# Second attention of a convolution-attention-expert network: heads inside images, keys projected three tiles after queries, image 0's softmax weights formed during image 1

## The reference, cut to what matters

```python
q, k, v = jnp.reshape(qkv, (3, b, n, d, h))        # b=2, n=1024, d=128, h=8
score = jnp.einsum('bnqh,btqh->bnth', q, k) * d ** (-0.5)
attn = jax.nn.softmax(score, axis=1)               # over the queries n
av = jnp.einsum('bnnh,bnqh->bnqh', attn, v)        # only the diagonal of attn
out = av.reshape(b, n, d * h) @ W0 + b0
t = t + out; t = t + ffn(layer_norm(t))
```

## Time and profile before

| what | us |
| --- | --- |
| median of 3 runs (446.90 to 447.89) | 447.43 |
| the profiled execution: time | 447.12 |
| its span, first to last instruction | 445.4 |
| PE busy, of the span | 399.7 |
| DVE busy | 322.2 |
| ACT busy | 300.5 |
| POOL busy | 92.8 |

### The profile page before, as it was taken

One profiled execution on the slowest core, in us unless ns is written; L12 is line 12 of the kernel. 1 busy time (PEld: TensorE's weight loads), 2 busy tenths in 40 slices (PEclk: granted clock), 3 DMA queues, 4 the chain that ended last, 5 costly groups with the idle time before them and its releaser, 6 DMA issues.

```text
span 445.4 us, 6582 instructions
## 1 busy us (share of the span) xinstructions
PE 399.7 (90%) x1919; PEld 316.0 (71%) x1919; DVE 322.2 (72%) x697; ACT 300.5 (67%) x576; POOL 92.8 (21%) x121
## 2 busy tenths in 40 slices
PE   1989779969999999999999999999939999839995
PEld 1678776947888888888888888888825775726763
DVE  2788853327889888898889888898963557467555
ACT  1476684338989999999999999999851001637750
POOL 8600002023104221232132320423010110142000
PEclk9999998879999999999999999999985999958995
DMA  7940000000000000000000000000000000000002
GB/s 271 353 123 2 1 1 0 1 0 1 1 1 1 2 0 0 0 0 0 0 0 0 0 0 0 0 0 1 1 0 0 0 0 1 0 1 0 2 0 96
DMA packets 3877, 9.60 MB, mean 22 GB/s; under 512 B 530, under 2 KB 1682, under 8 KB 3730
## 3 DMA queue, kind: packets, MB, share of 16 engines
q1 hardware_dynamic: 3426, 8.39, 5.5%
q10 hardware_dynamic: 432, 0.97, 0.6%
HBM read 8.31 MB, written 1.05 MB: 21 GB/s over the span
## 4 chain that ended last, share of the span: by engine, by line
PE 79%; DVE 12%; issue 4%; ACT 2%; DMA 1%; POOL 0%; POOLq 0%; DVEq 0%; ACTq 0%
PE ps L998 12%; PE ps L1035 12%; PE ps L1037 12%; PE ps L1036 12%; PE ps L1080 6%; PE ps L942 3%; PE ps L950 2%; PE ps L961 2%; DVE nmax_all L1393 2%; PE ps L906 2%; PE ps L1073 2%; PE ps L937 2%; PE ps L881 1%; DMA xq<-laid_x_queries 1%; PE ps L1132 1%
## 5 line engine op out<-in xcount | busy, mean ns | idle before, releaser
L1393 DVE TENSOR_REDUCE nmax_all<-ps 128x1024 f32 (+1 forms) x128 | 156.8, 1225 | 3.8 <-PE ps L1037 3.2
L715 ACT ACTIVATE exps<-ps,nmax_all 128x1024 bf16<-128x1024 f32 x128 | 143.6, 1132 | 11.4 <-DVE diag L1401 10.2
L1035 PE MATMUL ps<-qT_hi,kT_hi 128*128 128x512 f32 x256 | 104.2, 407 | 4.2 <-DVE kT_lo L1372 4.2
L1037 PE MATMUL ps<-qT_hi,kT_lo 128*128 128x512 f32 x256 | 100.2, 391 | 0.0
L1036 PE MATMUL ps<-qT_lo,kT_hi 128*128 128x512 f32 x256 | 100.1, 391 | 0.0
L483 POOL TENSOR_TENSOR qT_lo<-xq,qT_hi 128x1024 fp32r<-128x1024 f32 x16 | 38.5, 2405 | 126.2 <-ACT xq L693 126.2
L998 PE MATMUL ps<-xn,w_head 128*128 128x342 f32 (+3 forms) x256 | 60.0, 388 | 0.0
L1035 PEld LDWEIGHTS ps<-qT_hi,kT_hi 128*128 128x128 f32 x256 | 48.3, 189 | 15.7 <-issue 4.7
L1036 PEld LDWEIGHTS ps<-qT_lo,kT_hi 128*128 128x128 f32 x256 | 48.4, 189 | 11.0
L1037 PEld LDWEIGHTS ps<-qT_hi,kT_lo 128*128 128x128 f32 x256 | 48.3, 189 | 10.3
L998 PEld LDWEIGHTS ps<-xn,w_head 128*128 128x128 f32 x256 | 44.2, 195 | 11.3 <-issue 1.1
(11 more groups left out here) (204 smaller groups left out, 552.7 us busy)
## 6 DMA issues: line engine op xcount, KB each, us to landing
wqkv<-in_L_attn_Wqkv SPq DMA_DIRECT2D x1, 1536.0 KB, 6.4
xq<-laid_x_queries SPq DMA_DIRECT2D x2, 512.0 KB, 7.2
xk<-laid_x_keys SPq DMA_DIRECT2D x2, 512.0 KB, 8.3
x<-in_x SPq DMA_DIRECT2D x1, 1024.0 KB, 9.4
w<-in_L_ffn_W SPq DMA_DIRECT2D x1, 1024.0 KB
out<-conv_e SPq DMA_DIRECT2D x4, 256.0 KB, 2.0
band_sb<-laid_band ACTq DMA_DIRECT2D x1, 724.0 KB, 9.8
w<-in_L_attn_W SPq DMA_DIRECT2D x1, 512.0 KB, 7.3
```

The costliest lines, as they stand in the source:

```text
L715: a.activation(exps[:, scores % 2, :], slot(s), ACT.Exp, bias=nmax_all[:, at], accum_out=sum_all[:, at]).then_inc(exp_done, 1)
L1035: mm(tgt, kT_hi[:, b, rows_], qT_hi[:, b, cols_], start=True, stop=False)
L1037: last = mm(tgt, kT_lo[:, b, rows_], qT_hi[:, b, cols_], start=False, stop=True)
L1393: v.tensor_reduce(nmax_all[:, at_head(col)], slot(s), AX_X, ALU.max, negate=True)\
```

## The change

Heads go inside images: unit u is image u // 8, head u % 8, with buffers u % 2, and all 16 units are written out. Every PE job has a number in one list. The keys of the next unit are projected between tiles 3 and 4, ACT takes them ahead of the exponential of tile 3, DVE ahead of its maximum of tile 4. Queries stay ahead of tile 1 on PE and ACT.

```diff
-        wqkv = sb("wqkv", [P, 3, D, HEADS])
+        wqkv = sb("wqkv", [P, HEADS, 3, D])
...
-        LN_PARTS = [((0, 1, 2, 3),), ((0, 1, 2, 3),), ((0, 1, 2), (3,))]
+        LN_PARTS = [((0, 1, 2, 3),), ((0, 1), (2, 3)), ((0, 1, 2), (3,))]
...
+        UNITS = 2 * HEADS
+        def unit_jobs(u):
+            jobs = []
+            for n in range(TILES):
+                if n == 1 and u + 1 < UNITS:
+                    jobs.append(("queries", u + 1, 0))
+                if n == 4 and u + 1 < UNITS:
+                    jobs.append(("keys", u + 1, 0))
+                if (u, n) == TURN_AT:
+                    jobs.append(("turned", 0, 0))
+                jobs.append(("score", u, n))
+            return jobs
+        TURN_AT = (HEADS + 1, 4)
+        JOBS = [("queries", 0, 0), ("keys", 0, 0)] + [job for u in range(UNITS) for job in unit_jobs(u)]
+        def job_slot(job):
+            return JOB_AT[job] % SLOTS
+        SUMS_SLOT = (1, 0)
```

PE: what a job waits for, and the value stage (value_biases, broadcast and value_products take a unit now; score tiles and projections are as before, with `wqkv[:, h, j, :]` as weights):

```diff
+            def slot_free(g):
+                if g < SLOTS:
+                    return
+                kind, u, n = JOBS[g - SLOTS]
+                if kind == "score":
+                    pe.wait_ge(exp_done, u * TILES + n + 1)
+                elif kind == "keys":
+                    pe.wait_ge(k_split, u + 1)
+                elif kind == "queries":
+                    pe.wait_ge(q_full, 3 * u + 3)
+                else:
+                    pe.wait_ge(aT_sb, 1)
...
+            pe.wait_ge(aT_sb, 1)
+            pe.wait_ge(exp_done, UNITS * TILES - 3)
+            value_biases(0)
+            pe.wait_ge(exp_done, UNITS * TILES - 2)
+            broadcast(0)
+            pe.wait_ge(exp_done, UNITS * TILES - 1)
+            broadcast(1)
+            for u in range(UNITS):
+                if u == HEADS:
+                    value_biases(1)
+                value_products(u)
+                if u + 2 == HEADS:
+                    pe.wait_ge(aT_sb, 2)
+                if u + 2 < UNITS:
+                    broadcast(u + 2)
+                if u == 3:
+                    pe.wait_ge(exp_done, UNITS * TILES)
+                    turn(1, 2 * SUMS_SLOT[1], aT_ps)
+                if u == 11:
+                    pe.wait_ge(t1_ready, 3)
+                    channel_means(1, 0, t1, "mean", 2)
+                    channel_means(1, 1, t1, "mean", 3)
+                if u == 14:
+                    pe.wait_ge(LN[1]["centred"], 2)
+                    variances(1, 0, 2, 0)
+                    variances(1, 0, 2, 1)
```

ACT (evacuate_queries waits for the POOL remainder of the unit before, as before; the scale of the scores is now its immediate):

```diff
+            for u in range(UNITS):
+                for n in range(TILES):
+                    if n == 1 and u + 1 < UNITS:
+                        evacuate_queries(u + 1)
+                    if n == 3 and u + 1 < UNITS:
+                        evacuate_keys(u + 1)
+                    exponential(u, n)
+                    if (u, n) == (HEADS, 4):
+                        weights_exponential(0)
+                    if (u, n) == TURN_AT:
+                        take_turned(0, 2 * job_slot(("turned", 0, 0)))
+            weights_exponential(1)
+            take_turned(1, 2 * SUMS_SLOT[1])
```

DVE (weights_input: sum and reciprocal; weights_first: weight and first split; weights_next: subtraction and split; each for one image):

```diff
+            keys_remainder(0)
+            for u in range(UNITS):
+                for n in range(TILES):
+                    if n == 4 and u + 1 < UNITS:
+                        keys_remainder(u + 1)
+                    maximum(u, n)
+                    if (u, n) == (HEADS, 3):
+                        weights_input(0)
+                    if (u, n) == (HEADS, 5):
+                        weights_first(0)
+                    if (u, n) == (HEADS, 6):
+                        weights_next(0, 1, a_all, a_rest)
+                    if (u, n) == (HEADS, 7):
+                        weights_next(0, 2, a_rest, a_all)
...
+            for u in range(UNITS):
+                scale_tokens(u)
+                if u == 1:
+                    weights_input(1)
+                if u == 2:
+                    weights_first(1)
+                if u == 3:
+                    weights_next(1, 1, a_all, a_rest)
+                    weights_next(1, 2, a_rest, a_all)
+                if 9 <= u <= 11:
+                    add_values(0, u - 9)
+                if u in (13, 14):
+                    dve.wait_ge(t1_ready, 3)
+                    centre(1, u - 13, t1, u - 11)
```

More of the change, by code:

```diff
@@ L333, in build, with unit @@
         THIRDS = ((0, 22, 0), (22, 43, 2), (43, 64, 1))
[L335 to L350, removed]
-            jobs = []
[L352 to L358, removed]
-            return jobs
[L361 to L372, removed]
+        UNITS = 2 * HEADS
+        SLOTS = 4
+        def unit(u):
+            return u // HEADS, u % HEADS
+        def unit_jobs(u):
+            jobs = []
+            for n in range(TILES):
[6 more added lines that the diff above has]
+                jobs.append(("score", u, n))
+            return jobs
+        TURN_AT = (HEADS + 1, 4)
+        JOBS = [("queries", 0, 0), ("keys", 0, 0)] + [job for u in range(UNITS) for job in unit_jobs(u)]
+        JOB_AT = {job: g for g, job in enumerate(JOBS)}
+        def job_slot(job):
+            return JOB_AT[job] % SLOTS
+        SUMS_SLOT = (1, 0)
         block = ctx.enter_context(nc.Block())
@@ L510, in _ @@
[L510 to L522, removed]
@@ L678, in _ @@
             act.wait_ge(bq_ready, 1)
[L680 to L719, removed]
@@ L737, in _, with evacuate_keys @@
-            a.activation(x1[:, :], t1[:, :], ACT.Identity, bias=VEC["L1_ffn_beta"]).then_inc(t1_beta, 1)
-            for c in range(4):
+            def evacuate_keys(u):
+                b, h = unit(u)
+                act.wait_ge(job_ps, JOB_AT["keys", u, 0] + 1)
+                for lo, hi, j, _ in groups(1, b):
+                    a.activation(kT_hi[:, u % 2, lo:hi], slot(job_slot(("keys", u, 0)), lo, hi), ACT.Identity,
+                                 bias=bqkv[:, j, h:h + 1]).then_inc(k_hi, 1)
@@ new lines, in evacuate_queries @@
+            def evacuate_queries(u):
+                b, h = unit(u)
+                act.wait_ge(job_ps, JOB_AT["queries", u, 0] + 1)
+                if u:
+                    act.wait_ge(q_split, u)
+                for dst, signal in ((qT_hi[:, u % 2, :], q_hi), (queries_full, q_full)):
+                    for lo, hi, j, _ in groups(0, b):
+                        a.activation(dst[:, lo:hi], slot(job_slot(("queries", u, 0)), lo, hi), ACT.Identity,
+                                     bias=bqkv_q[:, j, h:h + 1], scale=SCORE_SCALE).then_inc(signal, 1)
```

411 lines of the change are left out of this document (191 added, 220 removed).

## The result

The changed kernel takes **457.85 us** (median of 4 runs, 457.13 to 458.81) against 447.66 for the kernel before on the same chip (446.90 to 448.31): ratio 1.023, interval 1.0204 to 1.0255. It is slower by 10.2. Forecast: 461.4, range 454 to 469. The profiled execution took 457.79 for a span of 456.1.

A forecast was written before the change was run, and what follows sets the result against it. PE bounds the kernel before at 14.37 us a unit; late keys make a 15.83 ring. 445.4 + 24.1 (stage) - 9.9 (handover) + 3.5 (products) - 3.7 (tail) = 459.4 span, + 1.7 + 0.3 = 461.4 us; range 454 to 469.

The forecast's parts named there:

- The ring: Attention units: late keys close a round through DVE, ACT and PE, 15.83 us a unit against PE's 14.37; forecast 83%.
- the slot ring: Attention unit: PE writes K into Q's slot, so waits for the whole query evacuation; this round sums to 15.83 us.
- its floor: Attention unit without the slot wait: ACT meets K only behind e1 and e2, a second round of 15.74 us.
- Its signs: Middle unit: 15.8 us long, DVE idle 2.8 behind the fourth maximum, PE below 95% at clock 1.00, stalling about 1.5.
- Loop hops: Attention unit: hops cost 0.1 us more inside the hardware loop; if all four did in the new code, ring 16.2.
- Image 0's chain: Units 8 to 10: first DVE piece hidden, three others 1.6 us; unit 9 19.7, unit 10 14.96, together 3.0 over the ring.
- Handover, products, tail: After attention: handover 3.9 us (-9.9), products 40.0 (+3.5), behind the products to the last chunk mean -3.7.
- The low spell: Products: one stretch of low PE clock after the handover's idle, taken as 1.5 us, bounds 0 and 2.7.
- Rule against row: ACT evacuations: skill's rule gives 0.47 us each, measured rows 0.43; by the rule 0.37 more a unit, sum near 466.
- The start: Stretch to the first score matmul: forecast unchanged at 95.0 us.
- Rival 1: Attention stage: PE keeps the pace, no ring closes, units stay at 14.37 us, 436.9 in time; chance 8%.
- Rival 2: Attention stage: short PE gaps lower the clock, projections at half clock add 1.7 us a unit, about 487; chance 7%.

The follow-up runs named there:

- the first experiment: The changed kernel with the next unit's keys back beside its queries, all else as changed: 439.22 us, 437.76 when repeated.
- keys one tile earlier: The changed kernel with the keys projected ahead of tile 3 on PE and taken ahead of the exponential of tile 2 on ACT: 451.6 us.
- two products late: The changed kernel, keys still late, without the third product of each score (the variant with less PE work): 465.14 us.
- the kernel that spreads the chain: The changed kernel with keys beside queries and image 0's DVE pieces behind m0 of units 8 to 11, turned weights taken in unit 12: 435.51 us.

## Why the prediction was right

It forecast slower by 14 and the kernel is slower by 10.2. Of the 3.3 us by which the span came out shorter (456.1 for 459.4), the stage is 2.3 and the start 1.4, which no part of the argument had; the rest is 0.4 the other way. Step by step:

- **The ring.** Right in mechanism: it closes through DVE, ACT and the keys, PE is off the chain, and both single-part experiments (439.2 without the late keys, 472.3 with nothing else) put the loss there. The sum was 15.83, measured 15.64. Two terms of it were mis-sized. A DVE tile takes 1.34 (171.18 to 172.52) when DVE doesn't wait for PE; the 1.36 of the earlier trace rows was PE's pace, not DVE's own: 0.08. The remainder takes 1.45 to the next maximum, not 1.54, which was its duration and not its distance: 0.09. And the slot ring, along which the 15.83 was added up, wasn't the longer of the two: PE sees the slot 0.05 after ACT's queries end (181.83 to 181.88), not 0.16, and with the measured links (and 1.94 for K and the hop behind it, as forecast) that ring comes to 15.54. What holds is the one that the prediction had as its floor, ACT's own order with e1 and e2 ahead of the keys, by 0.10. The floor of 15.74 less 0.17, plus 0.06 for e1 and e2 at 2.24, gives the 15.64, but for rounding. Twelve units of 0.19 are 2.3, as much as the stage came out shorter by.
- **Its signs.** "PE below 95%" did not show: the window lists PE as busy for 15.16 of 15.64, 97%, because each matmul is listed 0.16 past the next one's start. By starts the unit holds PE's 14.37 of work in 15.64, 92%, and its stalls are 1.27, not 1.5. DVE idles 2.5 behind m3, not 2.8.
- **Loop hops.** The dearer 16.2 was rightly not taken: written-out code shows 15.64, loop code about 16.0.
- **Image 0's chain.** Three DVE pieces on the ring were put at 1.6; they measure 1.84 (0.68, 0.55, 0.61), and units 9 and 10 cost 3.3 over the ring against 3.0. By PE's first score matmuls (236.51, 256.36, 271.10) unit 9 takes 19.85 and unit 10 14.74, forecast 19.7 and 14.96. The first piece was forecast hidden, and is. But it took 2.05 (229.68 to 231.73), not 1.2, and its cover was nearly used up, as the timeline of the kernel after shows (DVE, then POOL):

```profile
229.68 1.58 DVE L1372 TENSOR_TENSOR a_rest<-diag_all,nmax_all 128x64 f32<-128x64 f32 x1
231.19 0.54 DVE L1375 RECIPROCAL sum_all<-sum_all 128x64 f32<-128x64 f32 x1
232.35 1.53 DVE L1344 SCALAR_TENSOR_TENSOR kT_lo<-ps,cols,kT_hi 128x342 fp32r<-128x342 f32 x3 [0.62 <-ACT kT_hi L622]
...
228.82 2.36 POOL L449 TENSOR_TENSOR qT_lo<-xq,qT_hi 128x1024 fp32r<-128x1024 f32 x1 [13.27 <-ACT xq L634]
```

  Of the idle 2.8 in which it should lie, 0.62 was left. The turned weights did hold up PE in unit 9: its tile 7 begins at

```profile
254.87 0.50 PE L986 MATMUL ps<-qT_hi,kT_hi 128*128 128x512 f32 x1 [0.93 <-ACT aT L659]
```

- **Handover, products, tail.** 3.6, 40.4, 12.9 against 3.9, 40.0, 13.1. The low spell that was taken as 1.5, between 0 and 2.7, came (clock 0.72 from 350 to 354). It doesn't in every execution: the repeated first experiment ran its first product in 2.00, not 3.29. These three gain 10.2 together, forecast 10.1; they are what the first experiment keeps.
- **Rule against row.** Evacuations in a row took 1.28 and 1.29 for three (179.11 to 180.39 to 181.68), 0.43 each, so the row was the right one. By the rule of the Trainium skill (ScalarE: Activation LUTs, What ACT_TABLE_LOAD costs) one of 341 columns takes an estimated 0.47 and the ring is an estimated 0.37 longer, away from what was measured.
- **The start.** It is 1.4 shorter, forecast as unchanged. 1.2 of it stands at PE's first product with conv_ws already (11.75 before, 10.51 after), and 0.6 of that at DVE's first instruction, which waits for the DMA of xq (5.97 and 5.35). All ten traces of the changed kernel and its variants have 10.5 to 10.7 there, and the two of the kernel before and its variant 11.75, so it goes with the change; why isn't shown. Over the twelve traces the first score matmul lies between 93.6 and 97.1, and most of this spread arises ahead of 18 us. The timelines of PE in the changed kernel and in the first experiment:

```profile
15.22 1.10 PE L784 MATMUL ps<-xk,conv_ws 128*128 128x512 f32 x2
...
16.06 2.05 PE L783 MATMUL ps<-xk,conv_ws 128*128 128x512 f32 x2
```

  The pair of the same shape ahead of it (from 10.94) took 2.05 or 2.06 in both. In four traces (before, changed, keys one tile earlier, two products late) the second pair takes 1.10 or 1.11, and the first score comes at 95.03 or sooner; in the other eight it takes 2.05, and the first score comes at 95.8 or later. The rows give the granted clock as 1.00 from 14 to 18 us in both cases. What decides it stays open. The changed kernel and the first experiment are 2.6 us apart by the start alone (93.60 and 96.16), so small differences of single totals say little.
- **Rivals.** Rival 1 (PE keeps the pace, 436.9) nearly comes true without the late keys, 439.2. Rival 2 (the clock) didn't happen: 0.99 over the stage; it does in the variant with less PE work. The Trainium skill (TensorE: Matmul & The Clock Gate, A second HAM failure mode) tells of another kernel, in bf16, whose frequent short idles between groups of matmuls made the clock swing between its two levels. The changed kernel idles shortly in every unit too (0.45 ahead of the key projection) and stays at 0.99 to 1.00; the variant with less PE work, at 0.89 to 0.94 in windows of 30 us, agrees with it. How much idle is too much no run here shows.

## What to carry to other kernels

When work is moved to another place in a periodic schedule, add up the round that every late piece makes through all engines, back to itself one period later. If that sum is over the busiest engine's time it is the new period, though no engine is full. Add start-to-start distances from a stretch where the engine in question is itself late, since the pace of another engine can be hidden in them; and put long side chains into the one place of each period where their engine waits anyway, one piece a period.

## What was not expected of the hardware

- *Less work on PE made a kernel slower.* With a third of the score matmuls left out, PE was busy 24.8 and 23.6 us in two windows of 30 us, the granted clock there was 0.94 and 0.89, and the projection on the ring went from 2.00 to 3.61. With the same matmuls and another order PE was busy 181 of 200 us at 0.99 and 1.00, and the kernel gained 12.7 us.
- *A DVE instruction of 0.2 us can take 1.6.* The subtraction of 64 columns took 1.58 when it met POOL's query remainder, and ended with it (228.82 + 2.36 = 231.18, the reciprocal starts at 231.19). With no POOL instruction beside it, it took 0.22 in the kernel that spreads the chain and 0.23 for image 1 in the changed kernel:

```profile
349.29 0.23 DVE L1372 TENSOR_TENSOR a_rest<-diag_all,nmax_all 128x64 f32<-128x64 f32 x1
```

  The Trainium skill (SBUF — State Buffer, SBUF: two separate sides) says that DVE with two inputs in SBUF and a GpSimd instruction that reads SBUF share a pair of ports, which whichever starts first holds to its end. The row agrees. It was not tried on its own: no run here moved POOL's instruction alone.
